# First loads of a block kernel in another order: three tables asked for behind the first scaling of Q, the conditions of tiles 2 and 3 ahead of the shared weights

## The chip, the cores and the metric

The kernel runs on one core of a Trainium2 chip. The metric is the device time of one execution in microseconds. Of the kernel before there are three timed runs: 805.69, 805.79 and 806.53 us, with the median at 805.79 us.

The engines are named as the profile names them: PE multiplies matrices (PEld loads its weights), DVE is the vector engine, ACT the scalar engine, POOL the third elementwise engine, and SP only issues transfers. ACT and POOL issue transfers too. A name with a q (SPq, ACTq, DVEq) is the sequencer of an engine, which works through issues, waits and register work.

## The reference

One block of a network runs over 4096 tokens (64 sequences of 64) of width 256. In short:

```
c  = x @ weight[category of the sequence] + bias[category]      # a 256x256 matrix per sequence
Q, K, V = c @ W.T + b + c @ A.T @ B.T / 8                         # low-rank addition, 16 heads of 16
a  = softmax(Q K.T / 4 + slope * distance) @ V                    # within a sequence
x  = x + c + rezero * (a @ Wo.T + bo + low rank part)
t  = (x @ lora_A[language].T) @ lora_B[language].T + lang_embed[language]
ys = geglu(t @ Ws1 + bs1) @ Ws2 + bs2                             # shared expert
yr = the two best of 12 experts by t @ Wr + br, each geglu(t @ We1 + be1) @ We2 + be2, weighted
x  = x + ys + yr
```

## The kernel before

**Tiles and stages.** The tokens are cut into 32 tiles of 128 tokens (two sequences). In the attention stage, about the first 340 us, each tile goes through `tile_steps(i)` on every engine; the tiles are software-pipelined, so that PE's step for tile i also computes the conditioned input of tile i+2 (`condition`, line 1211) and Q, K and V of tile i+1. The merging of the first-layer weights with the low-rank language matrices is worked into the same steps (`merge`, `merge_pair`). Two later stages, the shared expert and the routed experts in 75 tiles, follow and last until the end.

**What sets the order.** Every engine has a program written out by hand, and runs it in order; semaphores tie the engines together. A transfer is asked for by the engine in whose program the `dma_start` stands, and lands later. There are two queues of plain transfers: SP's (the page's q1) and ACT's (q10). Each DMA adds 16 to a semaphore when it has landed.

**The first loads on SP** (lines 309 to 327): x of tile 0, the weights `wm` of K, the condition of tile 0, the weights of Q, the position table `alibi`, the weights of V, then `load_tile(1)`, the weights of the output projection (line 321; `PROJECTIONS = (1, 0, 2, 3)`, so this is `wm[3]`), `bs2`, the two blocks of the shared weights `ws1`, `be1`, and `load_tile(2)` and `load_tile(3)`. `load_tile(i)` asks for x of tile i (`load_x`, 256 KB) and for its condition: four register loads of category numbers, two matrices of 256 KB (line 293, `cond_w`) and two bias rows spread over 64 partitions (line 296, `cond_bias`, 64 KB each). From tile 2 on it first waits until the buffers are free: `sp.wait_ge(xbo_sb, i - 1)` and `sp.wait_ge(c_ok, i - 1)`.

**The first loads on ACT** (lines 538 to 546): small tables and, last, the six `rest_loads`, with one semaphore `d_rest`: `ba`, the late part of `consts` (280 KB), `lang_i`, `lang_b`, `a_rows` (64 KB, in_lora_a) and `aT` (112 KB, in_lora_aT). In the trace `arena`, `ps` and `stage` are large buffers of which the tables named in the code are parts.

**The work around tile 0.** On PE: `low_rank_products`, `condition(0)`, the transposes of c (line 1226), K, Q (line 1234) and V (line 1250) of tile 0, `condition(1)` (line 1219), then `tile_steps(0)`: `score(0)` (lines 1264, 1270), Q and K of tile 1, `router_rows` (line 1189), the transposes of the probabilities (line 1279), V of tile 1, `condition(2)`, `attend(0)` (line 1292); then `router_products` (lines 1207 and 1208) and `score(1)`. `score(1)` waits for `v_sb`, the spreading of V of tile 1 on DVE.

On DVE: `c_add(0)` (line 762), the low-rank additions to the weights of Q and V (line 748), `k_spread(0)` (line 767), `c_add(1)`, `v_spread(0)` (line 778), and `tile_steps(0)`: `shift(0)` (lines 795 and 797), then `lang_setup`, then `k_spread(1)`, `pT_copy(0)` (line 805), `sums(0)` (line 811), `v_spread(1)`. `lang_setup` is:

```python
low_rank_weight(3, PROJECTIONS[3])          # needs wm[3], lines 748 and 754
dve.wait_ge(d_rest, REST)
V.tensor_copy(tri_b[:, :], col["tri"]).then_inc(s_const, 1)
V.tensor_copy(lang_tmp, lang_b[:, :])
link(V.tensor_copy(lang_f, lang_i[:, :]))
...                                          # lang_hot, 4 instructions of line 882
lang_routers()                               # line 836, needs col["block"], releases router_products
```

`col["tri"]` and `col["block"]` lie in the late part of `consts`. On ACT, `q_copy(0)` (line 570) scales Q of tile 0, and the next step of ACT is `cT_copy(1)` (line 565).

## Time and profile before

| | |
|---|---|
| three timed runs | 805.69, 805.79, 806.53 us (median 805.79) |
| the profiled execution | 806.17 us, its span 804.4 us |
| PE busy | 783.6 us, 97% of the span |
| DVE, POOL, ACT busy | 575.9, 405.4, 294.3 us |
| granted clock of PE, mean | 0.996 |

The span runs from the first to the last instruction of the core in one profiled execution; its own time is 1.8 us above its span. All times within the trace are microseconds from the start of the span. A landing is the end of a transfer, counted from the start of its issue. The page shows PE as busy nearly everywhere but in its first slices, where also the DMA engines are fullest.

### The profile page before, as it was taken

The numbers are of one execution on the slowest core, as the hardware profiler recorded it, in microseconds if no ns is written. First come the engines' busy times: TensorE is split into PE (matmuls) and PEld (weight loads), VectorE is DVE, ScalarE is ACT, GpSimd is POOL, SyncE is SP. The second block draws the span as 40 slices with busy tenths as digits, with TensorE's granted clock in tenths as the row PEclk, the third lists the DMA queues.
The fourth block names the chain that finished last, engine by engine and source line by source line (L and its number), as shares of the span: only waits on it lengthen the run. The fifth ranks groups of instructions, "written<-read, shape, count | busy, mean of one in ns | idle before, by whom it ended". The sixth has DMA issues, their size and how long they took to land.

```text
span 804.4 us, 27682 instructions
## 1 busy us (share of the span) xinstructions
PE 783.6 (97%) x9379; PEld 658.2 (82%) x9380; DVE 575.9 (72%) x1350; ACT 294.3 (37%) x883; POOL 405.4 (50%) x511
## 2 busy tenths in 40 slices
PE   7999999999999999999999999999999999999994
PEld 6788888888888888777778888888888888888883
DVE  2999877777777777679884676666666666666661
ACT  1444444444444444542222333333333333333330
POOL 3133244444444444401012777777777777777762
PEclk9999999999999999999999999999999999999998
DMA  9553355555565554048734233223222322232222
GB/s 277 153 187 101 112 170 180 182 174 177 180 182 181 182 182 146 2 158 232 231 130 139 28 42 37 33 35 39 35 34 33 38 38 33 34 40 36 33 31 26
DMA packets 49325, 86.11 MB, mean 107 GB/s; under 512 B 7298, under 2 KB 27970, under 8 KB 49122
## 3 DMA queue, kind: packets, MB, share of 16 engines
q1 hardware_dynamic: 33778, 68.83, 27.2%
q0 software_dynamic: 13888, 15.13, 14.3%
q10 hardware_dynamic: 1584, 1.10, 0.5%
q8 instruction: 54, 0.88, 0.5%
q14 instruction: 21, 0.17, 0.1%
HBM read 68.48 MB, written 16.55 MB: 106 GB/s over the span
## 4 chain that ended last, share of the span: by engine, by line
PE 90%; DVE 5%; issue 2%; DMA 1%; SPq 0%; POOL 0%; ACT 0%; DVEq 0%
PE ps L1575 24%; PE ps L1562 13%; PE ps L1234 7%; PE ps L1473 6%; PE ps L1332 4%; PE ps L1556 4%; PE ps L1306 3%; PE ps L1250 3%; PE ps L1279 3%; PE ps L1462 3%; PE ps L1219 3%; PE ps L1543 2%; PE ps L1339 2%; PE ps L1292 2%; PE ps L1321 2%
## 5 line engine op out<-in xcount | busy, mean ns | idle before, releaser
L1575 PE MATMUL ps<-arena,stage 128*128 x900 | 206.6, 379 | 0.0
L1575 PEld LDWEIGHTS ps<-arena,stage 128*128 128x128 f32 x900 | 165.2, 190 | 19.5
L504 POOL DMA_INDIRECT out_dram<-stage,to_row x75 | 120.6, 1609 | 76.0 <-DVE stage L1143 71.3
L708 ACT ACTIVATE stage<-ps 128x384 f32<-128x384 f32 x150 | 65.4, 488 | 241.6 <-PE ps L1562 241.6
L1562 PE MATMUL ps<-token_rows,token_rows_T 64*128 64x128 f32 x1800 | 129.2, 272 | 0.0
L1562 PEld LDWEIGHTS ps<-token_rows,token_rows_T 64*128 64x128 f32 x1800 | 118.8, 188 | 1.7
L496 POOL DMA_INDIRECT token_rows<-gated_rows,from_row x75 | 75.1, 1001 | 61.6 <-DVE to_row L1022 38.9
L1117 DVE COPY token_rows<-ps 128x128 f32<-128x128 f32 x75 | 21.9, 292 | 111.8 <-PE ps L1544 111.8
L408 POOL TENSOR_TENSOR arena<-arena 128x256 f32<-128x256 f32 x32 | 23.4, 732 | 139.3 <-DVE arena L832 132.3
L1127 DVE TENSOR_TENSOR stage<-ps,stage 128x384 f32<-128x384 f32 x150 | 76.0, 549 | 1.8 <-ACT stage L708 1.8
L795 DVE TENSOR_REDUCE arena<-ps 128x8 f32<-128x512 f32 x64 | 43.9, 686 | 42.4 <-PE ps L1270 42.0
L1234 PE MATMUL ps<-arena 128*128 128x128 f32 x512 | 63.1, 276 | 0.9 <-ACT arena L565 0.8
L1556 PE MATMUL ps<-token_rows,token_rows_T 64*128 64x256 bf16 x450 | 62.1, 273 | 0.0
L1234 PEld LDWEIGHTS ps<-arena 128*128 128x128 f32 x512 | 59.7, 192 | 1.6 <-ACT arena L565 1.0
L1473 PE MATMUL ps<-ws,stage 128*128 128x256 f32 x256 | 59.1, 384 | 0.0
L578 ACT ACTIVATE arena<-arena 128x512 f32<-128x512 f32 x64 | 40.3, 630 | 50.0 <-DVE arena L797 49.7
L1473 PEld LDWEIGHTS ps<-ws,stage 128*128 128x128 f32 x256 | 47.4, 190 | 9.8 <-issue 4.0
L797 DVE TENSOR_TENSOR arena<-ps,arena 128x512 f32<-128x512 f32 x64 | 44.3, 691 | 2.2
L270 DVE COPY token_rows_T<-w_merged 128x256 f32 x75 | 44.7, 596 | 0.7 <-issue 0.7
L1119 DVE TENSOR_SCALAR token_rows<-ps,consts 128x128 bf16<-128x128 f32 x150 | 45.1, 343 | 0.0
L511 POOL COPY token_rows_T<-w_bias 128x384 bf16 x75 | 42.8, 570 | 0.9 <-issue 0.8
L590 ACT COPY arena<-arena 128x128 f32<-128x128 f32 x64 | 15.9, 295 | 73.4 <-DVE arena L817 73.4
(173 smaller groups left out, 1473.8 us busy)
## 6 DMA issues: line engine op xcount, KB each, us to landing
stage<-in_we_dram SPq DMA_DIRECT2D x36, 512.0 KB, 4.7
arena<-in_cond_w_dram SPq DMA_DIRECT2D x64, 256.0 KB, 2.8
arena<-in_we_dram SPq DMA_DIRECT2D x12, 768.0 KB, 6.0
arena<-in_x_both_dram SPq DMA_DIRECT2D x31, 256.0 KB, 2.7
arena<-in_L_cond_bias_dram SPq DMA_DIRECT2D x64, 64.0 KB, 2.9
out_dram<-arena SPq DMA_DIRECT2D x32, 128.0 KB, 2.7
be_bc<-in_be_rows_dram SPq DMA_DIRECT2D x13, 192.0 KB, 3.4
gated_rows<-token_rows POOLq DMA_DIRECT2D x2, 1152.0 KB, 11.6
```

The source lines that it names most:

```text
L270: copy(w1x[s % 2][:, j * CW:(j + 1) * CW], w1m[:, ds(e * (NJ * CW) + j * CW, CW)]).then_inc(w1x_ok[j], 1)
L496: pool.indirect_dma_start(s_row[s], None, gated_rows, bass.IndirectOffsetOnAxis(from_row[:, t:t + 1], 0)).then_inc(d_row[s], 16)
L504: pool.indirect_dma_start(out_rows, bass.IndirectOffsetOnAxis(to_row[:, t:t + 1], 0), y_sb[t % YR], None, compute_op=ALU.add).then_inc(d_a ...
L708: nc.scalar.activation(g_sb[hf].rearrange("p (j n) -> p j n", n=P), first_out[1][:, :, hf, :], ACT.Gelu).then_inc(g_ok, 1)
L797: V.tensor_tensor(probs[:, 512 * half:512 * half + 512].rearrange("p (g h k) -> p g h k", g=2, k=S), scores[:, banks], top.unsqueeze(3).to ...
L1119: last = V.tensor_scalar(s_langT[s % 2][:, hf * P:(hf + 1) * P], ps[:, 7, P:2 * P], col["half"][:, hf:hf + 1], None, ALU.mult)
L1127: V.tensor_tensor(actT_sb[s % 2][:, hf, :].rearrange("p (j n) -> p j n", n=P), first_out[0][:, :, hf, :], g_sb[hf].rearrange("p (j n) -> p ...
L1234: last = mm(ps[:, bank, at + m * P:at + (m + 1) * P], wm[w][:, k, m * P:(m + 1) * P], cT[:, k, :], start=(k == 0), stop=(k == KC - 1))
L1473: last = mm(ps[:, 4 + v, half * D:(half + 1) * D], sh_aT[half][:, k, v * P:(v + 1) * P], ws2[:, k, :], start=(k == 0), stop=(k == HS // P ...
L1556: mm(first_out[g][:, j].rearrange("p h n -> p (h n)"), w1bx[s % 2].bitcast(bf16)[64 * g:64 * g + 64, at], s_langT[s % 2][64 * g:64 * g + 6 ...
L1562: last = mm(first_out[g][:, j, hf, :], w1x[s % 2][64 * g:64 * g + 64, j * CW + hf * P:j * CW + (hf + 1) * P], s_rowT[s % 2][64 * g:64 * g ...
L1575: last = mm(ps[:, 4 + s % 2, 0:D], actT_sb[s % 2][:, hf, j * P:(j + 1) * P], arena[:, ds(e * E2 + (NJ * hf + j) * D, D)], start=(hf == 0 a ...
```

## The change

Three of the six `rest_loads` become `late_loads` with a semaphore `d_late` of their own, and are issued on ACT behind `q_copy(0)`. On SP, `load_tile(2)` moves ahead of the weights of the output projection, and `load_tile(3)` between the two blocks of `ws1`. On DVE, `lang_routers` and the copy of `tri` move out of `lang_setup` into `late_setup`, behind `sums(0)`, and wait for `d_late`; PE waits for it at the start of `router_products`.

```diff
-            (ba[:, :, :].rearrange("p c n -> p (c n)"), a["lora_ba"]), (consts[:, EARLY:], a["consts"][:, EARLY:]),
-            (lang_i[:, :], a["lang_of"]), (lang_b[:, :], a["lang_rows"]),
-            (a_rows, a["lora_a"]), (aT.rearrange("p c l n -> p (c l n)"), a["lora_aT"])]
+            (ba[:, :, :].rearrange("p c n -> p (c n)"), a["lora_ba"]), (lang_i[:, :], a["lang_of"]),
+            (lang_b[:, :], a["lang_rows"])]
+        late_loads = [
+            (consts[:, EARLY:], a["consts"][:, EARLY:]), (a_rows, a["lora_a"]),
+            (aT.rearrange("p c l n -> p (c l n)"), a["lora_aT"])]
+        LATE = 16 * len(late_loads)
...
             load_tile(1, True)
+            load_tile(2, False)
             n = PROJECTIONS[3]
             sp.dma_start(wm[n].rearrange("p c n -> p (c n)"), a["wT"][n]).then_inc(d_wT[n], 16)
             sp.dma_start(bs2_bc[:, :], a["bs2_rows"]).then_inc(d_bs2, 16)
-            for j in range(NJS):
-                load_first(j, a["ws1"][j])
+            load_first(0, a["ws1"][0])
+            load_tile(3, True)
+            load_first(1, a["ws1"][1])
             load_be1(0)
-            load_tile(2, False)
-            load_tile(3, True)
...
             q_copy(0)
+            for dst, src in late_loads:
+                act.dma_start(dst, src).then_inc(d_late, 16)
             tile_steps(0, between=routers_copy)
...
                 dve.wait_ge(d_rest, REST)
-                V.tensor_copy(tri_b[:, :], col["tri"]).then_inc(s_const, 1)
                 V.tensor_copy(lang_tmp, lang_b[:, :])
...
                 dve.wait_ge(s_hot, 1)
+
+            def late_setup():
+                dve.wait_ge(d_late, LATE)
                 lang_routers()
+                V.tensor_copy(tri_b[:, :], col["tri"]).then_inc(s_const, 1)
...
                 sums(i)
+                late()
...
-            tile_steps(0, False, lang_setup)
+            tile_steps(0, False, lang_setup, late_setup)
...
             def router_products():
+                pe.wait_ge(d_late, LATE)
                 pe.wait_ge(r_lang_ok, 1)
```

On DVE, in tile 0, from the second subtraction of `shift(0)` (line 797 before, 802 after) to `v_spread(1)`. Before:

```order
L797 TENSOR_TENSOR arena<-ps,arena 128x512
L748 SCALAR_TENSOR_TENSOR arena<-ps,arena 128x512
L754 TENSOR_SCALAR arena<-arena 128x512
L878 CAST tri_b<-consts 128x128
L879 CAST arena<-lang_b 128x64
L880 CAST arena<-lang_i 128x32
L882 TENSOR_SCALAR arena<-arena 128x32 x4
L836 TENSOR_TENSOR arena<-arena,consts 69x48
L767 SCALAR_TENSOR_TENSOR arena<-ps,arena,consts 128x256 x2
L805 COPY arena<-ps 128x512
L811 TENSOR_REDUCE arena<-arena 128x16
L778 TENSOR_TENSOR arena<-ps,arena 64x16x16 x2
```

The same stretch of the changed kernel:

```order
L802 TENSOR_TENSOR arena<-ps,arena 128x512
L753 SCALAR_TENSOR_TENSOR arena<-ps,arena 128x512
L759 TENSOR_SCALAR arena<-arena 128x512
L883 CAST arena<-lang_b 128x64
L884 CAST arena<-lang_i 128x32
L886 TENSOR_SCALAR arena<-arena 128x32 x4
L772 SCALAR_TENSOR_TENSOR arena<-ps,arena,consts 128x256 x2
L810 COPY arena<-ps 128x512
L816 TENSOR_REDUCE arena<-arena 128x16
L841 TENSOR_TENSOR arena<-arena,consts 69x48
L893 CAST tri_b<-consts 128x128
L783 TENSOR_TENSOR arena<-ps,arena 64x16x16 x2
```

The copy of `tri` and `lang_routers` moved from ahead of `k_spread(1)` to a place between `sums(0)` and `v_spread(1)`; the rest kept its order.

On SP, from the second bias row of the condition of tile 1 on (line 296 before). Before:

```order
L296 DMA arena<-in_L_cond_bias_dram 64x256
L321 DMA arena<-in_wT_dram 128x512
L322 DMA bs_bc<-in_bs_rows_dram 128x256
L282 DMA stage<-in_ws_dram 128x1024 x2
L307 DMA be_bc<-in_be_rows_dram 128x384
L288 DMA arena<-in_x_both_dram 128x512
```

In the changed kernel, from the second bias row of the condition of tile 2 on (line 299):

```order
L299 DMA arena<-in_L_cond_bias_dram 64x256
L325 DMA arena<-in_wT_dram 128x512
L326 DMA bs_bc<-in_bs_rows_dram 128x256
L285 DMA stage<-in_ws_dram 128x1024
L291 DMA arena<-in_x_both_dram 128x512
```

What follows the weights of the output projection is now `bs2`, one block of `ws1` and x of tile 3; x and the condition of tile 2, 896 KB in five transfers, moved ahead of them.

On ACT, the end of the first loads and the first steps on tiles 0 and 1. Before:

```order
L546 DMA ba<-in_lora_ba_dram 128x192
L546 DMA consts<-in_consts_dram 128x559
L546 DMA lang_i<-in_lang_of_dram 128x32
L546 DMA lang_b<-in_lang_rows_dram 128x64
L546 DMA arena<-in_lora_a_dram 64x256
L546 DMA arena<-in_lora_aT_dram 128x224
L565 ACT_TABLE_LOAD
L565 COPY arena<-ps 128x128 x2
L570 ACTIVATE arena<-ps,arena 128x128 x2
```

After:

```order
L549 DMA ba<-in_lora_ba_dram 128x192
L549 DMA lang_i<-in_lang_of_dram 128x32
L549 DMA lang_b<-in_lang_rows_dram 128x64
L568 ACT_TABLE_LOAD
L568 COPY arena<-ps 128x128 x2
L573 ACTIVATE arena<-ps,arena 128x128 x2
L643 DMA consts<-in_consts_dram 128x559
L643 DMA arena<-in_lora_a_dram 64x256
L643 DMA arena<-in_lora_aT_dram 128x224
```

Three issues moved behind `q_copy(0)` and now stand ahead of `cT_copy(1)`.

## Rows read from the trace of the kernel before

**Rows 1.** The page: the shares of the chain that ended last, by engine.

```profile
PE 90%; DVE 5%; issue 2%; DMA 1%; SPq 0%; POOL 0%; ACT 0%; DVEq 0%
```

**Rows 2.** The chain of waits, start and length in us, 5 to 28 us.

```profile
5.53 5.49 DMA arena<-in_L_cond_bias_dram
...
15.64 1.30 issue
16.94 1.10 PE ps L1219 x8
...
21.95 0.69 DVE arena L748
...
23.15 0.14 DVE tri_b L878
...
24.00 0.20 DVE arena L836
...
25.59 1.12 DVE arena L811
...
27.49 0.14 issue
27.63 0.32 PE ps L1264 x8
```

**Rows 3.** Stretches: us, busy PE, PEld, DVE, ACT, POOL, clock, DMA share, GB/s.

```profile
8.00:14.00 6.00, 4.13 (x43) 3.18 (x41) 1.56 (x4) 1.72 (x3) 1.45 (x2) 1.00 1.06 330
16.00:20.00 4.00, 2.70 (x54) 1.87 (x55) 1.86 (x4) 0.43 (x2) 0.72 (x1) 1.00 1.04 387
```

**Rows 4.** Issues asked window by window: size, then us from issue to landing.

```profile
consts<-in_consts_dram ACTq DMA_DIRECT2D x1, 279.5 KB, 5.1
arena<-in_lora_aT_dram ACTq DMA_DIRECT2D x1, 112.0 KB, 6.5
arena<-in_wT_dram SPq DMA_DIRECT2D x1, 256.0 KB, 3.1
arena<-in_wT_dram SPq DMA_DIRECT2D x1, 256.0 KB, 6.1
be_bc<-in_be_rows_dram SPq DMA_DIRECT2D x1, 192.0 KB, 6.4
```

**Rows 5.** SP's sequencer in order of time: start, length, line; issues only.

```profile
7.79 0.43 SPq L288 DMA_DIRECT2D arena<-in_x_both_dram  x1
9.53 0.90 SPq L293 DMA_DIRECT2D arena<-in_cond_w_dram  x2
11.83 0.58 SPq L321 DMA_DIRECT2D arena<-in_wT_dram  x1
12.93 2.00 SPq L282 DMA_DIRECT2D stage<-in_ws_dram  x2
14.98 0.43 SPq L307 DMA_DIRECT2D be_bc<-in_be_rows_dram  x1
18.29 1.19 SPq L296 DMA_DIRECT2D arena<-in_L_cond_bias_dram  x2
```

**Rows 6.** Landings (least, median, most) of cond_w of tile 1, then cond_bias of tile 2.

```profile
DMA to landing us min/median/max: 5.6/6.2/6.8
...
DMA to landing us min/median/max: 4.6/5.0/5.4
```

**Rows 7.** Engines in order of time: PE's `condition(2)` and router products; ACT.

```profile
24.26 1.08 PE L1219 MATMUL ps<-arena 128*64 128x256 f32 x8
26.28 0.64 PE L1207 MATMUL ps<-arena 64*128 64x48 f32 x4
26.85 0.42 PE L1208 MATMUL ps<-arena 5*128 5x48 f32 x2
14.67 0.63 ACT L570 ACTIVATE arena<-ps,arena 128x128 f32<-128x128 f32 x2 [2.10 <-PE ps L1234]
19.16 0.43 ACT L565 COPY arena<-ps 128x128 f32<-128x128 f32 x2 [3.87 <-PE ps L1226]
```

More of the change, by code:

```diff
@@ L207, in adaln_attn_moe @@
             "p (j h n) -> p j h n", h=2, n=P) for g in range(2)]
-        d_cat, d_first, d_near, d_ali, d_rest, d_low, d_first_x, d_bs2, d_zero = [sem(n) for n in (
-            "d_cat", "d_first", "d_near", "d_ali", "d_rest", "d_low", "d_first_x", "d_bs2", "d_zero")]
+        d_cat, d_first, d_near, d_ali, d_rest, d_late, d_low, d_first_x, d_bs2, d_zero = [sem(n) for n in (
+            "d_cat", "d_first", "d_near", "d_ali", "d_rest", "d_late", "d_low", "d_first_x", "d_bs2", "d_zero")]
         d_wT = [sem(f"d_wT{c}") for c in "qkvo"]
@@ L890, in router_setup, with tile_steps @@
                 lang_part(0)
-            def tile_steps(i, odd, between=lambda: None):
+            def tile_steps(i, odd, between=lambda: None, late=lambda: None):
                 one_more, two_more = not isinstance(i, int) or i + 1 < NT, not isinstance(i, int) or i + 2 < NT
```

## The prediction

> **What bounds the kernel now.** I read the chain of waits first, as shares and then in order of time, since only its pieces can move the end. By shares it is PE for 90% [rows 1]: over nearly the whole span PE has its own work ahead of it. The first 28 us are different, and the change touches only these. There the chain [rows 2] begins with a transfer, the second bias row of tile 0, issued at 5.53 and landed 5.49 later, at 11.02. PE then does K, Q and V of tile 0 and is through at 15.64. Now it has nothing for 1.30 us, until `condition(1)` (line 1219) starts at 16.94. The row calls this "issue"; what it waits for is found in the issues. The two matrices of the condition of tile 1 are issued at 9.53 and take 0.90 together, so the second issue starts near 10.0 [rows 5], and the longest landing of the pair is 6.8 [rows 6]: 16.8 to 16.9, where `condition(1)` starts. From its end the chain is on DVE (`c_add(1)`, `v_spread(0)`, `shift(0)`, `lang_setup` from 21.95 on, and so to `v_spread(1)`), until `score(1)` starts on PE at 27.63 [rows 2]. From there on the events of the pipeline follow from one another on PE and DVE. A gain that is there when `score(1)` starts is passed on to the end; one that is lost before it is lost.
>
> Two views say why a 256 KB transfer takes over 6 us here. The stretch from 8 to 14 us has a DMA share of 1.06 at 330 GB/s, and that from 16 to 20, when only SP's queue still has much in it, 1.04 at 387 GB/s [rows 3]: the 16 DMA engines are full. The first of four such loads took 3.1 us from issue to landing, and the last one, of the output projection's weights, 6.1 [rows 4]. So a byte taken out ahead of another moves that one forward, and a byte put ahead moves it back.
>
> **The three tables leave the front.** They are 280, 64 and 112 KB: 456 KB, or 0.467 MB. In the trace `consts` is issued third last but four on ACT and has landed 5.1 after its issue, the last one, `aT`, 6.5 after its [rows 4]; both before the condition of tile 1 has landed, so all three were carried ahead of its second matrix. At the 330 GB/s of that stretch they cost 0.467/0.330 = 1.41 us; at 387 it would be 1.21. The second matrix then lands at 16.85 - 1.41 = 15.44, and with the same 0.1 us of reaction `condition(1)` can start at 15.53. PE must be through with V of tile 0 by then. It is: `consts` alone, carried ahead of the bias row that starts the chain, is 286 KB, 0.87 us, so PE comes free near 14.8. Even if that row did not come earlier at all, PE would be free at 15.64, and the gain would be 1.30 instead of 1.41. So `condition(1)` comes 1.41 us earlier (1.2 to 1.65; the upper end if many small transfers cost more than their bytes), and with it all of DVE's chain up to the end of `shift(0)`.
>
> **The weights of the output projection come later.** This is the price. The first instruction of `lang_setup`, line 748 at 21.95 [rows 2], needs `wm[3]`. Before, it was issued at 11.83 [rows 5] and landed 6.1 later [rows 4], at 17.93, four microseconds ahead of need. Now x and the condition of tile 2 stand in front of it: 256 + 512 + 128 = 896 KB. What these cost is in the trace: `be1` is issued at 14.98 [rows 5] and lands 6.4 later [rows 4], at 21.4; behind it follow exactly these five transfers, of which the last, the second bias row, is issued near 18.9 (the pair starts at 18.29 and takes 1.19, rows 5) and lands 5.4 later [rows 6], at 24.3. That is 2.95 us. The three tables do not help here: they leave the front but come back before this load. ACT issues them behind `q_copy(0)`, which ended at 15.30 [rows 7] and now ends about 0.7 earlier, at 14.6; SP reaches line 321's load at 11.83 plus the 4.04 of one `load_tile` (7.79 to 11.83, rows 5), at 15.9. So all 456 KB are in the other queue while SP's works through tile 2. `wm[3]` lands at 17.93 + 2.95 = 20.9. The lower bound is the same 0.917 MB at 387 GB/s, 2.4 us, 20.3. An upper bound is 24.3, where tile 2's condition landed with `bs2`, both blocks of `ws1` and `be1` (1.3 MB) ahead of it too; I take 20.9, since it leaves out just what is no longer ahead, and allow 0.4 either way.
>
> DVE wants it at 21.95 - 1.41 = 20.54, and gets it at 20.9 + 0.1 = 21.0. So DVE waits for 0.45 us, with `k_spread(1)`, `pT_copy(0)`, `sums(0)` and `v_spread(1)` queued behind and `score(1)` waiting for them. Of the 1.41 there remains 21.95 - 21.0 = 0.95. Note that this no longer depends on how much the condition of tile 1 gained.
>
> **The moved instructions of DVE.** `tri` is 0.14 and line 836 0.20 of the chain [rows 2]. Both leave the place ahead of `k_spread(1)` and come back ahead of `v_spread(1)`, which waits for the same sum of work: nought. But `router_products` on PE, 0.99 us long (26.28 to 27.27, rows 7), waits for line 836 and stands ahead of `score(1)`. Before, `sums(0)` ended at 26.71 [rows 2]; without the 0.34 it ends at 26.37, line 836 at 26.57, and with the 0.14 from DVE to PE (the row at 27.49) the products run from 26.71 to 27.70, against 27.63 for `score(1)` before. That is 0.07, and one more wait on DVE's queue some 0.04: I take 0.1; between nought and 0.34 (nothing overlaps).
>
> **The late tables themselves.** Issued from 14.6 to about 16.2 and slow as `aT` was (6.5), they are there by 22.7; line 836 wants them near 25.6. The cover is 2.9 us. The three issues occupy ACT until 16.2, and its next step, `cT_copy(1)` at 19.16 [rows 7], comes at 17.7 now: 1.5 us of cover. An issue can be held up when the queue is deep: the two of `ws1` took 2.00 together [rows 5], against the 0.43 of another. One such hold, 1.1 us, is covered on ACT, and on SP too, where it would put the issue of `wm[3]` at 17.0, and 3.1 us after that is still before 20.9.
>
> **The conditions of tiles 2 and 3.** `condition(2)` ran at 24.26 [rows 7], right behind PE's other work, and the bias row behind its matrices landed at 24.3. PE was not held by it, though there was little room. With the new order it lands near 20. It is insurance, worth nothing in the sum unless PE comes forward by more than the 0.95. `load_tile(3)` waits for `c_add(1)` and stands ahead of `ws1`'s second block and `be1`, which are wanted in tile 2's merge, over 15 us later. Tile 3's own condition is wanted a whole tile later than tile 2's. Cover: several microseconds each.
>
> **Sum.** 1.41 - 0.45 - 0.10 = 0.86 us. The profiled execution is 806.17, 0.38 above the median of the timed runs; its span of 804.4 would become 803.5, and the median 805.79 - 0.86 = 804.9.
>
> **A rule of the skill beside the trace.** Rows first: the same 256 KB took 3.1 us on queues that had just been opened and 6.1 behind others [rows 4]. The Trainium skill, in "DMA: Bandwidth & Descriptors", section "Anatomy of one DMA", gives a transfer as a fixed part of about 2.0 us plus its bytes at 436 GB/s (fitted to the GpSimd path), an estimate of 2.6 us for this one. By that rule, counted from the issue at 15.9, the weights would land at 18.5, no wait would arise on DVE, and the result would be the first rival's. The trace contradicts it while the engines are full, by 3.5 us for the row at 6.1. The same page, section "Queues, rings and completion order", says that each DMA engine takes turns between the queues that have work. By it the late tables do not stay behind the weights because SP asked earlier, which is what the sum has; the sum would be 1.4 us kinder to `wm[3]` if the two queues did not share.
>
> **The rivals.**
> 1. No wait on DVE. If `wm[3]` lands by 20.4, the whole 1.41 is kept, less 0.1: 804.5. For it: the lower bound of 20.3, and the 3.1 us of an uncrowded load. Against it: the late tables come back in this very stretch, and the 2.95 measured for the same five transfers.
> 2. The new order is the bottleneck: `wm[3]` lands after 21.86, the point from which DVE starts `lang_setup` later than before. It needs only one more of the late tables' length than I count, or a hold of SP's queue with idle DMA engines behind it. If it lands at 22.9 the kernel loses 1.1 us: 806.9; the upper bound of 24.3 gives 808.3.
> 3. The tables bring nothing forward, because the matrices of tile 1 are limited by SP's queue alone and not by the bytes beside it. Then `shift(0)` ends as before, the load still has the 2.95 ahead of it and the late tables too, 20.9 to 22.3, for a need at 21.95: 805.8 to 806.2. Against it: the share of 1.06 in that stretch.
> 4. More comes than the bytes say: 1.65 for the tables, `wm[3]` in time, and no loss at the router: 804.1.
>
> **How the numbers follow.** The forecast has 0.55, with an own range of 804.4 to 805.4. Rival 1 has 0.21, rival 2 0.08, rival 3 0.09, rival 4 0.07. The range of 804.1 to 806.0 holds the forecast, rivals 1 and 4 and about half of the third. 0.2% is 1.6 us, about what a measurement of this kernel can tell from no change. Faster than 804.2 needs rival 4 in full or a low median: 0.08. Slower than 807.4 needs the far half of rival 2: 0.04, with 0.01 for what I did not see. So 0.87 for within 0.2%.
>
> **What would show it.** In the chain of the changed kernel, `condition(1)` starts near 15.5 and not at 16.9. The first instruction of `lang_setup` (line 753 now) has idle time before it of 0.2 to 0.8 us, ended by the DMA of `wT`, and starts near 21.0. `score(1)` starts near 26.8. Every later mark, such as the first tiles of the routed stage, is earlier by the same amount. The forecast is wrong if `condition(1)` starts after 16.5 (the tables were not what it waited behind), if line 753 has no idle time before it (rival 1) or starts after 21.95 (rival 2), or if a gain at `score(1)` is gone by 60 us, for which I see no row.

## The result, and the profile after

| | before | changed |
|---|---|---|
| median of the timed executions | 805.72 us (13 executions, 805.01 to 806.53) | 807.16 us (13 executions, twelve of them 806.13 to 808.72) |
| profiled execution | 806.17 us, span 804.4 | 808.17 us, span 806.4 |
| start of `condition(1)` | 16.94 us | 15.33 us |
| start of the first instruction of `lang_setup` | 21.95 us | 21.17 us |
| start of `score(1)` | 27.63 us | 27.22 us |
| start of a group of 16 matmuls near 340 us | 340.19 us | 342.35 us |

The thirteenth execution of the changed kernel took 1314.88 us at an average clock of 0.556, and the ratio leaves it out; the median of the other twelve is 807.00. The ratio is 1.0018 with an interval of 1.0010 to 1.0027. So the changed kernel is slower, by 1.4 us; that is within the 0.2% that the prediction called no change, but its 804.9 and its range of 804.1 to 806.0 were both missed.

The page of the changed kernel, its line of busy times, the clock line of 40 slices, and the shares of the chain that ended last:

```profile
PE 786.8 (98%) x9379; PEld 661.0 (82%) x9380; DVE 578.0 (72%) x1350; ACT 294.6 (37%) x883; POOL 405.8 (50%) x511
...
PEclk9899999999999999999999999999999999999997
...
PE 90%; DVE 5%; issue 2%; SPq 2%; DMA 1%; POOL 0%; DVEq 0%; ACT 0%
```

The shares are those of before [rows 1]. What is new is one digit: the second slice, 20 to 40 us, has an 8 where all its neighbours have a 9. The granted clock was below full speed somewhere in it. First, though, the chain in order of time (start, length, what), beside [rows 2]:

```profile
16.84 4.23 DMA arena<-in_wT_dram
21.17 0.70 DVE arena L753
...
24.58 1.12 DVE arena L816
25.70 0.12 DVE arena L841
25.83 0.14 issue
25.96 0.67 PE ps L1217 x4
26.64 0.59 PE ps L1218 x2
27.22 0.37 PE ps L1274 x6
...
29.49 3.71 PE ps L1244 x16
33.20 0.93 PE ps L1316 x4
...
342.35 3.47 PE ps L1483 x16
```

Up to 27.22 this is the forecast. The weights of the output projection land at 21.07, DVE goes on at 21.17, `sums(0)` (line 816) and the moved routers (line 841) follow, the two groups of router products stand ahead of `score(1)` (line 1274), and `score(1)` is 0.41 us earlier than before. Six microseconds later the gain has become a loss. Here are the same places of the kernel before:

```profile
29.14 2.05 PE ps L1234 x16
31.20 0.87 PE ps L1306 x4
...
340.19 3.47 PE ps L1473 x16
```

Line 1234 of before is line 1244 now, 1306 is 1316, 1473 is 1483. From `score(1)` to line 1306 the kernel before took 31.20 - 27.63 = 3.57 us; the changed one took 33.20 - 27.22 = 5.98 from `score(1)` to line 1316. That is 2.41 us more for the same work, and 16 matmuls that took 2.05 take 3.71. The chain names no wait there. From 33.20 (2.00 late) on little more is lost: 2.16 at 342 us, and 2.0 at the end of the span. The stretches of the changed kernel tell why (stretch, length, busy PE, PEld, DVE, ACT, POOL, granted clock, DMA share, GB/s):

```profile
24.00:26.00 2.00, 0.69 (x33) 0.59 (x33) 2.00 (x5) 0.00 (x0) 0.74 (x2) 1.00 0.91 196
26.00:28.00 2.00, 2.00 (x38) 1.82 (x46) 1.39 (x4) 0.50 (x2) 0.00 (x0) 0.59 0.82 308
28.00:30.00 2.00, 2.00 (x28) 1.34 (x15) 1.38 (x3) 0.80 (x3) 0.00 (x0) 0.50 0.08 31
30.00:34.00 4.00, 4.00 (x20) 3.85 (x20) 1.71 (x3) 1.89 (x4) 0.00 (x0) 0.60 0.02 4
34.00:40.00 6.00, 6.00 (x134) 4.95 (x133) 5.38 (x13) 1.80 (x6) 2.14 (x3) 1.00 0.44 130
```

Here is 26 to 28 us of the kernel before:

```profile
26.00:28.00 2.00, 1.64 (x61) 1.39 (x58) 1.92 (x5) 0.20 (x1) 0.00 (x0) 1.00 0.28 98
```

PE's granted clock is 1.00 (2.4 GHz) until 26, 0.50 (1.2 GHz) all through 28 to 30, and back at 1.00 from 34. It was busy for only 0.69 of the 2 us ahead of the fall. Two rows of PE in order of time (start, length, engine, line, tile, shape, idle time before it and what ended it), and DVE's first one of `lang_setup`, show what left it idle:

```profile
11.80 1.44 SPq L291 DMA_DIRECT2D arena<-in_x_both_dram  x1
...
16.84 0.59 SPq L325 DMA_DIRECT2D arena<-in_wT_dram  x1
...
15.33 1.09 PE L1229 MATMUL ps<-arena 128*64 128x256 f32 x8 [0.75 <-issue]
...
21.17 0.69 DVE L753 SCALAR_TENSOR_TENSOR arena<-ps,arena 128x512 f32<-128x512 f32 x1 [0.76 <-DMA arena<-in_wT_dram]
...
24.68 0.65 PE L1302 MATMUL ps<-arena 128*32 128x64 f32 x32 [0.95 <-issue]
25.96 0.67 PE L1217 MATMUL ps<-arena 64*128 64x48 f32 x4 [0.63 <-DVE arena L841]
```

The first gap is that of `attend(0)` (line 1302): it is 0.95 us, since PE has done `condition(2)` early and DVE, held for 0.76 by the weights, brings the probabilities late. The same gap was 0.35 before. The second is new: the router products wait 0.63 for line 841, which now stands behind `sums(0)`. Together PE idles 1.58 of the 2.24 us from 23.72, the end of `condition(2)`, to 25.96. So the theory was: the order brought two short idles of PE into one stretch; PE's clock then fell to half from about 26.4 to 33.2 us, and this costs more than the whole gain. Its rival: the load order itself costs the time, through late transfers, and the clock is an accident of one execution.

### The profile page after: what moved, and what is told of

It is laid out like the page before. It is cut to its first block, busy times and chain, and to the rows that moved or that the text cites. A ratio compares the mean times of both kernels' runs of the same rounds, so it can differ in the third digit from the quotient of the medians.

```text
span 806.4 us, 27684 instructions
## 1 busy us (share of the span) xinstructions
PE 786.8 (98%) x9379; PEld 661.0 (82%) x9380; DVE 578.0 (72%) x1350; ACT 294.6 (37%) x883; POOL 405.8 (50%) x511
## 4 chain that ended last, share of the span: by engine, by line
PE 90%; DVE 5%; issue 2%; SPq 2%; DMA 1%; POOL 0%; DVEq 0%; ACT 0%
PE ps L1585 24%; PE ps L1572 12%; PE ps L1244 7%; PE ps L1483 6%; PE ps L1342 4%; PE ps L1566 4%; PE ps L1316 3%; PE ps L1260 3%; PE ps L1289 3%; PE ps L1472 3%; PE ps L1229 3%; PE ps L1553 2%; PE ps L1349 2%; PE ps L1302 2%; PE ps L1331 2%
## 5 line engine op out<-in xcount | busy, mean ns | idle before, releaser
L1244 PE MATMUL ps<-arena 128*128 128x128 f32 x512 | 64.8, 281 | 0.8 <-ACT arena L568 0.8
L1244 PEld LDWEIGHTS ps<-arena 128*128 128x128 f32 x512 | 61.4, 196 | 1.6 <-ACT arena L568 0.9
L593 ACT COPY arena<-arena 128x128 f32<-128x128 f32 x64 | 15.9, 295 | 74.2 <-DVE arena L822 74.2
```

The source lines that it names most:

```text
L1244: last = mm(ps[:, bank, at + m * P:at + (m + 1) * P], wm[w][:, k, m * P:(m + 1) * P], cT[:, k, :], start=(k == 0), stop=(k == KC - 1))
```

## Experiments

In each block below every kernel ran beside the kernel before on the same chip. Ratios are to that one, with the 95% interval. Besides the medians I use a count: how many of the timed executions had a granted clock, averaged over the whole span, of 0.992 or less. The averages of executions whose profile shows no fall were 0.995 to 0.997; the two with a long fall had 0.990 and 0.992. A shorter one had 0.994, and such are not counted. The count is rough for another reason too: the average holds the last microseconds of the span, where the clock differs from profile to profile (790 to 801 us: 0.83 in the kernel before, 0.96 with the late tables alone, 0.68 in the first run with the gaps filled). The kernel before had 6 of 139 such executions in the four blocks of the experiments, the changed kernel 8 of 12 in the first measurement.

### The two halves of the change alone

The late tables without the new order of SP:

```diff
             load_tile(1, True)
-            load_tile(2, False)
             n = PROJECTIONS[3]
             ...
-            load_first(0, a["ws1"][0])
-            load_tile(3, True)
-            load_first(1, a["ws1"][1])
+            for j in range(NJS):
+                load_first(j, a["ws1"][j])
             load_be1(0)
+            load_tile(2, False)
+            load_tile(3, True)
```

> Change: the three late tables on ACT behind q_copy(0) and the moved DVE instructions, as in the changed kernel, but SP's loads in the order of the kernel before (the output projection's weights ahead of bs2, ws1 and tile 2). Theory A (the weights of the output projection, put behind tile 2, make DVE wait 0.76 us; PE then idles 0.95 us before attend(0) and 0.63 us before the router products, and the granted clock falls to its lower level for some 7 us, which costs 2.9): here DVE does not wait for wT, condition(1) starts near 15.3, score(1) near 26.3, no lower clock near 26 us, time 804.4. But tile 2's matrices, now behind 1.3 MB, could hold condition(2). Theory B (moving the router products behind sums(0) is what opens PE's gap, whatever DVE waits for): the gap before the router products stays and the lower clock too, 806 to 807. Theory C (the two late tables crowd the queues): as the changed kernel, 807.

The new order of SP without the late tables: in the kernel before,

```diff
             load_tile(1, True)
+            load_tile(2, False)
             n = PROJECTIONS[3]
             ...
-            for j in range(NJS):
-                load_first(j, a["ws1"][j])
+            load_first(0, a["ws1"][0])
+            load_tile(3, True)
+            load_first(1, a["ws1"][1])
             load_be1(0)
-            load_tile(2, False)
-            load_tile(3, True)
```

> Change: SP's loads in the new order, all six rest tables on ACT at the front as before, DVE and PE as before. Theory A: condition(1) at 16.9 as before; the weights of the output projection land near 20.9 and are wanted at 21.95, so DVE waits little or not at all; 805.7, no lower clock near 26 us. Theory B: as before, 805.7. Theory C: as before. If the new SP order is bad in itself (ring full, x of tile 2 held), DVE starts lang_setup after 22.2 and the time is 806.2 or more.

| kernel | median, us | ratio | clock at most 0.992 |
|---|---|---|---|
| before, this chip | 806.16 | | 3 of 35 |
| late tables alone | 806.77 | 1.0006 [0.9996, 1.0015] | 4 of 11 |
| new order of SP alone | 806.37 | 1.0004 [0.9995, 1.0013] | 1 of 11 |

Neither half alone is told from no change. With the late tables alone, DVE starts `lang_setup` at 19.26 without a wait, 2.7 us ahead of before, and still nothing is won. Its chain and PE's `condition(2)` say why, with two stretches:

```profile
15.38 7.85 DMA arena<-in_x_both_dram
...
24.68 1.35 PE L1229 MATMUL ps<-arena 128*64 128x256 f32 x8 [2.89 <-issue]
...
24.00:26.00 2.00, 1.32 (x12) 0.64 (x16) 1.04 (x4) 0.50 (x2) 0.00 (x0) 0.84 0.85 250
26.00:28.00 2.00, 2.00 (x38) 1.74 (x37) 0.42 (x1) 0.00 (x0) 0.00 (x0) 0.50 0.36 112
```

x of tile 2, asked for behind the shared weights, lands 7.85 us after its issue, at 23.23, and PE stands idle for 2.89 before `condition(2)` at 24.68. `condition(2)` also waits for the two matrices of tile 2, asked for at 17.16, behind x; they are the likely cause of the last 1.44 us, but the trace has no landing for them. This idle too is followed by the lower clock. So the second half of the change is no mere insurance: in this profile, once the tables come forward, tile 2's loads are what PE waits for. Alone, that half costs nothing that can be seen: with the new order alone, DVE finds the weights there (line 748 starts at 20.92 directly behind `shift(0)`), and the time is that of before. Its price, DVE's wait for the weights, appears only when the tables come forward as well.

### The weights ahead of tile 2

In the changed kernel, one load is moved:

```diff
             load_tile(1, True)
-            load_tile(2, False)
             n = PROJECTIONS[3]
             sp.dma_start(wm[n].rearrange("p c n -> p (c n)"), a["wT"][n]).then_inc(d_wT[n], 16)
+            load_tile(2, False)
```

> Change: the changed kernel, but the output projection's weights are asked for ahead of load_tile(2) again; everything else as in the changed kernel. Theory A: no wait of DVE for wT, shift(0) ends near 20.4, score(1) near 26.3, no lower clock near 26 us, time 804.4 (1.3 us below the kernel before). Theory B: PE still idles 0.6 us before the router products behind sums(0), the clock falls as in the changed kernel in part of the executions, 806 to 807.

It gave 805.22 against 806.16, 0.9985 [0.9975, 0.9994], with 2 of 12 executions at the low average. DVE has no wait before line 753 and PE none before line 1302, which starts at 24.70. The gap before the router products is still there, 0.63, and the clock does not fall in this profile (1.00 in every stretch from 20 to 40 us). With the first gap closed in this way the loss is gone, and the kernel is 0.9 us below before. The time lies between the two that had been expected, 804.4 and 806 to 807.

### The gaps filled with work

The changed kernel with matmuls on a tile of ones (`warm`, which the kernel already uses at its start; the result is never read) in the two gaps, and with every wait kept. The fills need one wait more on PE, for the copy of the bank of `ps` that they write into:

```diff
                 if two_more:
                     condition(i + 2, odd)
+                fill()
                 ...
+            def fill_gap():
+                pe.wait_ge(s_sp1c, 1)
+                warm(15)
+
-            tile_steps(0, False, 0, between=router_rows)
+            tile_steps(0, False, 0, between=router_rows, fill=fill_gap)
             pe.wait_ge(s_sp1c, 1)
+            warm(8)
```

This is the experiment that separates the clock from the loads: it moves no transfer and no step of DVE, and it can only add work and a wait to PE.

> Change: the changed kernel with 15 small matmuls on ones (60 ns each at the upper level) on PE behind condition(2), ahead of attend(0), and 8 ahead of the router products; they compute nothing that is used. DVE still waits 0.76 us for wT. Theory A: the idle time of PE is filled, the granted clock stays at its upper level, score(1) near 26.9, time 805.0. Theory C (the clock is only a symptom, the time is lost to the loads): no change against the changed kernel, 807.2.

It gave 804.55 against 806.16: 0.9981 [0.9973, 0.9990], with 0 of 11 executions at the low average. I ran it again beside the changed kernel itself, and with each gap filled alone:

> The changed kernel itself, as the measure for the three others of this call on one chip: 806 to 808, with a part of the executions at a mean clock of 0.992 or less.

> The changed kernel with 15 small matmuls on ones in PE's first gap (ahead of attend(0)) and 8 in the second (ahead of the router products); they compute nothing that is used. If the clock is the whole loss: 804.5, no execution at 0.992 or less, 1.5 to 3 us below the changed kernel of this call, and 0.8 to 1.6 below the kernel before.

> Only the 15 small matmuls in the first gap, ahead of attend(0). If the first gap brings the lower clock: as with both filled, 804.5. If the second does or both must be filled: between it and the changed kernel, some executions at 0.992 or less.

> Only the 8 small matmuls in the second gap, ahead of the router products. If the first gap brings the lower clock: as the changed kernel, 806 to 808. If the second does: 804.5.

| kernel, all on one chip | median, us | ratio | clock at most 0.992 |
|---|---|---|---|
| before | 806.39 | | 1 of 35 |
| changed | 807.55 | 1.0014 [1.0002, 1.0026] | 4 of 12 |
| changed, both gaps filled | 804.55 | 0.9987 [0.9978, 0.9995] | 0 of 12 |
| changed, only the one before line 1302 | 805.92 | 0.9999 [0.9988, 1.0011] | 2 of 12 |
| changed, only the one before the router products | 805.85 | 1.0001 [0.9987, 1.0016] | 2 of 12 |

23 useless matmuls make the changed kernel 3.0 us faster; the two intervals do not touch. DVE's first instruction of `lang_setup`, PE in order of time with both fills, and the stretch:

```profile
20.69 0.69 DVE L753 SCALAR_TENSOR_TENSOR arena<-ps,arena 128x512 f32<-128x512 f32 x1 [1.53 <-DMA arena<-in_wT_dram]
...
22.41 1.01 PE L1192 MATMUL ps<-ones_b 128*128 128x128 bf16 x15
24.20 0.65 PE L1302 MATMUL ps<-arena 128*32 128x64 f32 x32 [0.78 <-issue]
24.79 0.62 PE L1192 MATMUL ps<-ones_b 128*128 128x128 bf16 x8
25.48 0.61 PE L1217 MATMUL ps<-arena 64*128 64x48 f32 x4
26.39 0.32 PE L1274 MATMUL ps<-arena 2*64 2x256 bf16 x8
...
26.00:28.00 2.00, 1.86 (x48) 1.38 (x47) 1.62 (x5) 0.92 (x5) 0.00 (x0) 1.00 0.34 129
```

DVE waits here longer for the weights (1.53) than in the first profile (0.76), and the kernel is still the faster one. With no transfer moved and the wait for it still there, the rival, that the load order itself costs the time, is ruled out. The first gap is only filled in part: 15 matmuls take 1.01 us of it, and 0.78 of idle is left before line 1302. So this idle alone was not followed by the fall. The profile of the changed kernel in the same block has both gaps and a fall, a shorter one:

```profile
24.69 0.65 PE L1302 MATMUL ps<-arena 128*32 128x64 f32 x32 [1.67 <-issue]
25.97 0.61 PE L1217 MATMUL ps<-arena 64*128 64x48 f32 x4 [0.63 <-DVE arena L841]
...
28.00:30.00 2.00, 2.00 (x16) 1.57 (x9) 1.66 (x3) 1.06 (x4) 0.00 (x0) 0.50 0.00 0
30.00:34.00 4.00, 4.00 (x36) 3.68 (x36) 2.79 (x8) 2.39 (x6) 0.72 (x1) 0.97 0.02 4
```

With only one of them filled, 2 of 12 executions stay at the low average, and by the medians about half of the 3.0 us is won. That both gaps count is indicated and not shown: the intervals of these two kernels overlap with that of the changed kernel and with that of both fills, and 2 of 12 is not told from 4 of 12.

Would the fills help the kernel before as well, whatever its gaps?

> Change: the kernel before with the same 15 and 8 small matmuls in the same places on PE, which compute nothing that is used. Theory A says the kernel before suffers from a lower clock only rarely: 0 to 0.5 us faster. If the small matmuls are what wins by themselves, 1.5 us faster, 804.5.

They do not: 806.03 against 805.94, 1.0000 [0.9991, 1.0009]. PE's gaps there were short (0.35 before line 1292), and the fills do not fit into them: in the profile of this run `score(1)` starts 11.77 us after `condition(1)`, where the kernel before has 10.69. So the fills do not make a kernel faster by themselves. That there was nothing to win is not shown, since a gain of up to that microsecond could be hidden behind their own cost.

### The changed kernel again

> The changed kernel itself, unchanged, beside the others on one chip. If the lower clock comes in part of the executions (theory A), its times spread over some 3 us, those with a mean clock of 0.992 or less above 807 and those of 0.995 or more near 805; median 806.5 to 807.5.

> The changed kernel itself once more. Theory A (the lower clock comes in part of its executions only): of 11 or 12 executions some 3 to 8 have a mean clock of 0.992 or less and take 807.5 or more; the others 805 to 806.3.

| block | before, us | changed, us | ratio | clock at most 0.992 |
|---|---|---|---|---|
| first measurement | 805.72 | 807.16 | 1.0018 [1.0010, 1.0027] | 8 of 12 |
| second | 805.94 | 805.92 | 1.0008 [0.9996, 1.0021] | 2 of 12 |
| third | 806.35 | 807.90 | 1.0007 [0.9996, 1.0017] | 4 of 11 |
| fourth | 806.39 | 807.55 | 1.0014 [1.0002, 1.0026] | 4 of 12 |

In the second and third block the ratio is not told from 1, and the median of the second, 805.92, is below the 806.5 to 807.5 that was expected. (The ratio is not the quotient of the medians, which in the third block is 1.0019.) In the third block the times fall into two groups: 805.00, 805.87 and 806.27, and then eight executions from 807.61 to 808.15. Only four of these eight are at 0.992 or less, the others at 0.993 and 0.994, so the average clock alone does not sort them. The profiled execution of that block was the 805.00, and has the gaps without the fall:

```profile
21.24 0.69 DVE L753 SCALAR_TENSOR_TENSOR arena<-ps,arena 128x512 f32<-128x512 f32 x1 [0.72 <-DMA arena<-in_wT_dram]
...
24.74 0.65 PE L1302 MATMUL ps<-arena 128*32 128x64 f32 x32 [0.92 <-issue]
26.02 0.61 PE L1217 MATMUL ps<-arena 64*128 64x48 f32 x4 [0.63 <-DVE arena L841]
26.93 0.32 PE L1274 MATMUL ps<-arena 2*64 2x256 bf16 x8
...
30.33 1.03 PE L1316 MATMUL ps<-arena 128*128 128x256 f32 x4
...
28.00:30.00 2.00, 1.86 (x17) 1.62 (x16) 1.97 (x4) 1.34 (x4) 0.00 (x0) 1.00 0.04 8
```

Its waits and gaps are those of the first profile to within 0.04 us, its clock stays at 1.00 (2.4 GHz), and its span is 803.2 against 806.4. Of these 3.2 us between two executions of one program, most are the clock in this stretch: from `score(1)` to line 1316 this one takes 30.33 - 26.93 = 3.40 us, exactly what the kernel before takes in the same view (27.63 to 31.03), and the first profile took 5.84 (27.15 to 32.99). The profile of the second block has the gaps too (0.87 and 0.63), no fall, and a span of 802.0. The same gaps can go either way, then; they give the fall its chance and do not force it.

### Without the gaps: routers early, weights first

The second gap can be removed without filling it. The three tables land by 19.0 us (below), so `lang_routers` can go back to `lang_setup`, and only the copy of `tri` stays behind `sums(0)`:

```diff
                 dve.wait_ge(s_hot, 1)
+                dve.wait_ge(d_late, LATE)
+                lang_routers()
 
             def late_setup():
-                dve.wait_ge(d_late, LATE)
-                lang_routers()
                 V.tensor_copy(tri_b[:, :], col["tri"]).then_inc(s_const, 1)
```

This edit alone, then together with the weights ahead of tile 2 (twice), and the weights ahead of tile 2 together with the fills:

> Change: the changed kernel with lang_routers back in lang_setup (waiting for d_late there), the weights of the output projection still behind load_tile(2). DVE still waits about 0.8 us for wT. If the two causes add (the wait for wT, and PE's second gap and order behind sums(0)), score(1) starts 0.5 to 0.7 us earlier than in the changed kernel, the gap before the router products is gone, the one before attend(0) stays: 804.7 to 805.3, with fewer executions at the lower clock than the changed kernel but some. If the wait for wT alone brings the lower clock, as the changed kernel.

> Change: the output projection's weights ahead of load_tile(2), and lang_routers back in lang_setup ahead of k_spread(1), where it now waits for d_late; only the copy of tri stays behind sums(0). Theory B (a good part of the loss is the gap of 0.63 us that PE has because the router products wait for a DVE instruction behind sums(0)): the gap is gone, the products follow attend(0) at once as in the kernel before, fewer executions at the lower clock, median 0.3 to 1 us below the variant with only the weights moved (805.2). Theory A alone (only the wait for wT counts): the same 805.2.

> The version with the output projection's weights ahead of load_tile(2) and lang_routers back in lang_setup, once more: 803.5 to 804.5, at most two executions at 0.992 or less, 1.5 to 2 us below the kernel before.

> Change: the output projection's weights ahead of load_tile(2), and the 15 and 8 small matmuls on ones in PE's two gaps, which compute nothing that is used. Theory A: neither a wait for wT nor a lower clock; score(1) 0.5 to 0.8 us earlier than with the small matmuls alone, median 803.5 to 804.2. If the loads are not the limit any more, the same 804.5 as with the small matmuls alone.

| kernel | before, us | median, us | ratio | clock at most 0.992 |
|---|---|---|---|---|
| routers early | 806.35 | 805.65 | 0.9986 [0.9976, 0.9996] | 1 of 12 |
| routers early, weights first | 805.94 | 804.02 | 0.9980 [0.9969, 0.9991] | 0 of 12 |
| the same again | 806.35 | 804.37 | 0.9980 [0.9968, 0.9992] | 0 of 12 |
| weights first, gaps filled | 805.94 | 804.40 | 0.9980 [0.9969, 0.9989] | 0 of 11 |

Routers early with the weights first has the lowest ratio of the versions that add no useless work: 0.2% faster than before, clear of the noise both times. Its rows:

```profile
21.61 0.20 DVE L841 TENSOR_TENSOR arena<-arena,consts 69x48 f32<-69x48 f32 x1
...
23.30 0.65 PE L1302 MATMUL ps<-arena 128*32 128x64 f32 x32 [0.22 <-issue]
23.88 0.64 PE L1217 MATMUL ps<-arena 64*128 64x48 f32 x4
25.37 0.32 PE L1274 MATMUL ps<-arena 2*64 2x256 bf16 x8 [0.50 <-DVE arena L783]
```

Line 841 is done long before PE wants it, the router products follow `attend(0)` without a gap, and `score(1)` starts at 25.37, 2.3 us ahead of before. Gaps filled (804.40) and gaps closed (804.02 and 804.37) come to the same time, which fits one cause cured in two ways.

The profiled execution of routers early alone is a late starter. The 36 matmuls on ones at its start took 98 ns each, 3.53 us together, against 61 ns, 2.18 together, in the third block's profile of the changed kernel; both rows of the stretch from 4 to 8 us show a clock of 1.00, so what slowed them is not shown. The row says little there: in both profiles the first 40 matmuls on ones took 111 ns each (4.45 us together), also under a clock of 1.00. `condition(1)` then starts at 16.33, and this execution took 807.47, where the median is 805.65. The profiles of the weights ahead of tile 2 (`condition(1)` at 16.20) and of the delayed DVE below (17.20) start late in the same way. Such a start is not seen in the average clock, and it is a second reason not to judge by single profiles.

### A delay of DVE in the kernel before

In the kernel before, one reduction whose result is not used is put at the head of `lang_setup`, to price a delay of DVE alone:

```diff
             def lang_setup():
+                V.tensor_reduce(rsum, lrows[:, 0:H, 0:NLR], AX.X, ALU.add)
```

> Change: the kernel before with one more DVE instruction at the start of lang_setup (a sum over 16 x 64 zeros into a scratch that is written again later, about 1.2 us), which stands for a wait of that length and computes nothing that is used. Theory A: score(1) starts 1.2 us later, PE idles longer before attend(0), and part of the executions fall to the lower clock near 27 us, which adds 2 to 3 us in each: 807.0 where none falls, 808.5 or more at the median. If a wait of DVE costs only its own length: 807.1, and the clock as in the kernel before.

```profile
22.20 1.21 DVE L876 TENSOR_REDUCE arena<-token_rows 128x16 f32<-128x1024 f32 x1
...
27.07 0.65 PE L1293 MATMUL ps<-arena 128*32 128x64 f32 x32 [1.48 <-issue]
```

It cost 2.8 us (809.18 against 806.35, 1.0029 [1.0018, 1.0041]) for an instruction of 1.21, and it opens PE's gap before `attend(0)` to 1.48. The median is the one expected by the theory, but not for its reason: only 2 of 11 executions were at the low average, and the profile shows no fall. In that profile `score(1)` starts at 29.01, 1.38 later than before, and the group of matmuls near 340 us 1.35 later (341.38 against 340.03, PE in order of time); the other 1.1 of its 2.5 us come behind that. So up to 340 us the delay cost about its own length. A gap of 1.48 alone was not followed by a fall here. What the other 1.6 us of the median are is open.

## Why the prediction was wrong, point by point

**The tables cost what was said.** `condition(1)` starts at 15.33, 1.61 us earlier, where 1.41 (15.5) was forecast. Part of this difference of two profiles is scatter: the new order of SP alone, which leaves everything ahead of `condition(1)` as it was, had it at 15.92. Without the late starters, the three profiles with the tables at the front have it at 15.92 to 16.94 (mean 16.35), and twelve with the tables late at 14.06 to 15.43 (mean 14.61). The mechanism stands and its size fits; the third rival, that the tables bring nothing, is refuted.

**The weights landed where the sum put them,** at 21.07 against 20.9, and DVE waited for 0.76 against 0.45. (The 2.95 us of the sum for tile 2's transfers is 2.9 by the landings it is worked out from, 24.3 less 21.4.) Three terms were each a little off. The issue of the weights came at 16.84 and not at 15.9, because x of tile 2 took 1.44 to issue, where the same issue had taken 0.43; this hold was priced (1.1 us) and called covered, as it nearly was: the transfer took 4.23 instead of 5.0. That the landing came within 0.2 us of the sum is thus in part luck: an issue 0.9 later and a transfer 0.8 shorter nearly cancel. And `shift(0)` ended at 20.41 and not at 20.54. In other executions of the changed kernel the wait was 0.67, 0.72 and 1.47. The first rival (no wait) and the second (after 21.86) did not occur.

**The late tables were no trouble.** Their landings after issue (KB, us):

```profile
consts<-in_consts_dram ACTq DMA_DIRECT2D x1, 279.5 KB, 2.9
...
arena<-in_lora_aT_dram ACTq DMA_DIRECT2D x1, 112.0 KB, 4.4
...
arena<-in_wT_dram SPq DMA_DIRECT2D x1, 256.0 KB, 4.2
```

`consts` is issued at 13.66 and `aT` at 14.62, so all are there by 19.0, where 22.7 was allowed. The cover of the prediction was larger than it reckoned; this is what made the routers early possible.

**The rule for one transfer.** 256 KB of weights took 3.1 and 6.1 us before [rows 4], and those of the output projection take 4.2 now. The Trainium skill, in "DMA: Bandwidth & Descriptors", section "Anatomy of one DMA", has a fixed part plus the bytes (fitted to the GpSimd path). By that rule, an estimate of 2.6 us, there would have been no wait on DVE. The trace contradicts it again, now by 1.6 us, at a DMA share of 0.92 from 16 to 20 us and 0.95 from 20 to 24.

**The router products behind `sums(0)`** were priced at 0.1 of delay and called nought otherwise. In time that is right where the clock does not fall: in the third block's profile the gain is 0.71 at line 753 and still 0.70 at `score(1)`. In the first profile 0.78 at line 753 became 0.41 at `score(1)`, because the router products themselves ran into the fall: line 1218 took 0.66 us there and 0.42 in the third block's profile. What was not seen is that the wait of 0.63 falls on PE, and right behind the other gap.

**The second half was called insurance, worth nothing in the sum.** With the late tables alone PE idles 2.89 us for tile 2 in the one profile, and nothing is won: it belonged in the sum as soon as the tables came late.

**The step that failed** is the sentence "A gain that is there when `score(1)` starts is passed on to the end". It took PE's speed as given. In the profiled execution PE's clock went to its lower level (1.2 GHz) shortly before `score(1)` and stayed there to 33.2, which turned 0.41 gained into 2.00 lost. Without the fall the sentence holds: the third block's profile is 0.70 ahead at `score(1)`, 0.70 at line 1316, 0.58 near 340 us and 1.2 at the end of the span. The prediction had named a gain at `score(1)` that is gone by 60 us as a sign of being wrong, and had given it no row and no price. The prediction looked at PE's gaps only for what they delay and never for what they do to its clock, though the gaps could have been computed from the terms in the sum: DVE held for 0.45 where PE was earlier by 1.41, and the wait for line 841. With both gaps filled the kernel runs 1.6 and 1.8 us below before in two blocks, both on one chip; the 0.86 forecast for the sum was, if anything, too little.

**What stays open.** Why the same gaps are followed by a fall in one execution and not in another. Why even the four executions of the first measurement above 0.992 were at 806.1 to 806.6, above before, while in the second block those ten have a median of 805.45, 0.5 below before; shorter falls, as in the fourth block's profile (0.994), and late starts are parts of it, but I did not separate them. Over its four measurements the changed kernel has a median of 807.95 in the 18 executions at 0.992 or less and 806.34 in the other 29, where the kernel before has 806.12 in its 133 above 0.992: the counted falls explain the loss against before, and not why nothing of the forecast gain is left in the rest. And what the rest of the 2.8 us of the delayed DVE is.

## What to carry to other kernels

When an edit shortens one engine's wait, compute the idle time that it opens on the matrix engine as well, and read the granted clock of those stretches before and after: here two idles of 1.6 us together were followed by 2.4 us of loss in the work behind them. Where the cause is in doubt, fill the gap with useless matmuls and keep all else; that separates the price of the clock from that of the wait in one run. And move transfers in the order in which their users come to need them once the edit is in, not in the order of before: here the weights and tile 2's loads each became the late one in turn.

## What the runs showed of the hardware that I had not expected

- Two idles of PE, 0.95 and 0.63 us, within 2.24 us, in a stretch with 0.69 of 2 us busy, were followed by a clock of 0.50 for most of 7 us, in about four executions of ten (18 of 47 at the low average). With 15 and 8 matmuls of 128x128 in them it was 0 of 23.
- A single idle of 1.41 us (only the second gap filled) or 1.48 us (DVE delayed) was not followed by a fall in its profile; one of 2.89 us (late tables alone) was.
- The issue of x of tile 2 on SP's queue, at 11.80 directly behind the loads of tile 1, took 1.44 us, where that of x of tile 1 had taken 0.43. The weights, issued five us later than before, landed sooner after their issue, 4.2 us instead of 6.1. Why the issue was held no run shows.
- The same kernel's `condition(1)` started anywhere from 14.60 to 15.43 us in four profiles. In three profiles of other versions the 36 matmuls on ones at the start took 92 to 98 ns each, where they took 61 in these four, under the same granted clock of 1.00.
